# A windowed attention's probabilities turned by VectorE and bounced through DRAM, their low part taken by GpSimd, and weights loaded in pieces

## The reference

```
qkv = h @ w_qkv                      # h: gated x, 8 x 128 x 512
scores = einsum('bqhgd,bkhd->bhgqk', q, k) * 128**-0.5
bias = -slopes * sqrt(max(rel, 0)), -inf where rel < 0
attn = softmax(scores + bias)
out = einsum('bhgqk,bkhd->bqhgd', attn, v).reshape(8, 128, 4096)
x = x + out @ w_o
```

## Time and profile before

| | |
|---|---|
| device time, median of 3 runs | 2028.7 us (2025.08 to 2028.84) |
| device time of the profiled execution | 2021.16 us |
| its span | 2018.5 us |
| TensorE busy | 1966.2 us, 97% |
| VectorE, ScalarE, GpSimd busy | 76%, 65%, 47% |
| mean granted TensorE clock | 0.998 |

### The profile page before, as it was taken

One profiled execution on the slowest core, in us unless ns is written; L12 is line 12 of the kernel. 1 busy time (PEld: TensorE's weight loads), 2 busy tenths in 40 slices (PEclk: granted clock), 3 DMA queues, 4 the chain that ended last, 5 costly groups with the idle time before them and its releaser, 6 DMA issues.

```text
span 2018.5 us, 35965 instructions
## 1 busy us (share of the span) xinstructions
PE 1966.2 (97%) x12221; PEld 1669.4 (83%) x12221; DVE 1536.3 (76%) x3386; ACT 1317.0 (65%) x3796; POOL 940.4 (47%) x917
## 2 busy tenths in 40 slices
PE   7999999999999999999999999999999999999997
PEld 6777777888888888888888888888888888888774
DVE  6777765667666656688887887888878878888997
ACT  4676773545544545567777777777777777777785
POOL 3200014565665665644544544545445445454662
PEclk9999999999999999999999999999999999999999
DMA  7301102333433334412121121121211211212010
GB/s 263 100 28 48 54 1 82 118 100 95 140 96 97 123 102 77 129 42 82 32 64 53 33 84 32 32 84 32 64 53 33 84 32 32 84 33 84 29 31 37
DMA packets 91158, 142.21 MB, mean 70 GB/s; under 512 B 24914, under 2 KB 63058, under 8 KB 86498
## 3 DMA queue, kind: packets, MB, share of 16 engines
q1 hardware_dynamic: 69474, 89.55, 13.4%
q0 software_dynamic: 21504, 50.37, 8.7%
HBM read 119.93 MB, written 19.93 MB: 69 GB/s over the span
## 4 chain that ended last, share of the span: by engine, by line
PE 85%; DVE 7%; ACT 4%; DMA 2%; issue 2%; SPq 0%; POOL 0%; ACTq 0%; DVEq 0%
PE PS L1721 9%; PE PS L1733 9%; PE PS L1633 8%; PE PS L1499 8%; PE PS L1556 8%; PE PS L1706 6%; PE PS L1688 6%; PE PS L1647 4%; PE PS L1512 4%; PE PS L1691 3%; PE PS L345 3%; PE PS L1527 3%; PE PS L1542 2%; PE PS L501 1%; PE PS L1657 1%
## 5 line engine op out<-in xcount | busy, mean ns | idle before, releaser
L1304 POOL DMA_INDIRECT ffn_weights<-in_kcache,arena x256 | 259.8, 1015 | 78.0 <-issue 77.1
L2626 POOL DMA_INDIRECT vcache<-in_vcache,rows x256 | 249.9, 976 | 77.1 <-issue 55.6
L2475 ACT ACTIVATE pr<-pr,sm 128x640 f32<-128x640 f32 x256 | 209.4, 819 | 64.6 <-DVE sm L2085 64.4
L2101 DVE TENSOR_TENSOR prT_lo<-PS,prT_hi 128x512 fp32r<-128x512 f32 x320 | 208.8, 685 | 42.0 <-ACT prT_hi L2486 25.4
L2486 ACT ACTIVATE prT_hi<-PS 128x512 fp32r<-128x512 f32 x320 | 178.0, 597 | 67.9 <-PE PS L1706 67.8
L2085 DVE CUSTOM_DVE_ANT_0 pr<-PS,ffn_weights,sm 128x640 f32<-128x640 f32 x256 | 211.0, 878 | 0.5 <-PE PS L1691 0.5
L2632 POOL TENSOR_TENSOR vcached_lo<-vcache,vcached_hi 128x512 fp32r<-128x512 f32 x64 | 83.3, 1301 | 235.8 <-ACT vcached_hi L2457 235.8
L1706 PE MATMUL PS<-consts,pr 128*128 128x128 f32 x1280 | 172.1, 273 | 1.4 <-DVE prT_lo L2101 1.2
L1706 PEld LDWEIGHTS PS<-consts,pr 128*128 128x128 f32 x1280 | 149.6, 141 | 25.2 <-DVE prT_lo L2101 1.9
L1688 PE MATMUL PS<-kT_hi,qT_hi 128*128 128x320 f32 x512 | 155.2, 311 | 3.8 <-DVE sm L2085 2.4
L1688 PE MATMUL PS<-kT_lo,qT_hi 128*128 128x320 f32 x512 | 154.1, 309 | 0.0
(11 more groups left out here) (324 smaller groups left out, 6446.3 us busy)
## 6 DMA issues: line engine op xcount, KB each, us to landing
arena<-in_wqkv SPq DMA_DIRECT2D x16, 1536.0 KB
arena<-in_wo SPq DMA_DIRECT2D x16, 1024.0 KB
turned_keys<-ffn_weights POOLq DMA_DIRECT2D x64, 256.0 KB
kcache<-turned_keys SPq DMA_DIRECT2D x256, 64.0 KB
arena<-in_wcT SPq DMA_DIRECT2D x8, 1024.0 KB, 6.4
ffn_weights<-in_kcache,arena POOLq DMA_INDIRECT x256
vcache<-in_vcache,rows POOLq DMA_INDIRECT x256
arena<-in_xT SPq DMA_DIRECT2D x8, 256.0 KB, 7.8
```

Source lines behind the costliest of these rows:

```text
L1304: pool.indirect_dma_start(out=key_pages[:, n % 2, c, :], out_offset=None, in_=T["kcache"], in_offset=bass.IndirectOffsetOnAxis(ap=key_rows ...
L2101: dve.tensor_tensor(prT2[1][:, n % 3, :, :].rearrange("p h n -> p (h n)"), bank(4 + n % 2), prT2[0][:, n % 3, :, :].rearrange("p h n -> p ...
L2475: act.activation(pr2[:, h, :], pr2[:, h, :], ACT.Exp, bias=nm2[:, h:h + 1], scale=-1.0, accum_out=rs2[:, h:h + 1]).then_inc(a2_ex, 1)
L2626: pool.indirect_dma_start(out=vcache[:, c, :], out_offset=None, in_=T["vcache"], in_offset=bass.IndirectOffsetOnAxis(ap=rows[:, g, b, c:c ...
```

## The change

For items 8 to 54 (`TURNED`, 47 items) TensorE no longer turns the probabilities. VectorE transposes them in 32x32 blocks right after it has normalised them, SyncE stores the result to DRAM (256 KB, one transfer) and loads it back in four transfers of 64 KB so that the blocks land where a full transposition puts them; the queries then stand in the order (block, head, query), and `hi_of_o1` and `lo_of_o1` read them accordingly. ScalarE rounds the landed tile one step later than before, ahead of its copy of the turned key. The low part is taken by GpSimd instead of VectorE: in its list it stands behind the store of the step's last unit of keys and the first of the four gathers that follow it. `weigh1` of item i moves into TensorE's step i+1, between the second and the third quarter of the query head, and `project_out1` of item i into step i+2. The own values get a third buffer for that. The low parts of the output weights are taken in the second step of a group instead of the first. SyncE's list is written anew: the weights of a group come in pieces of 128 columns, spread over the steps behind each item's bounce. Items before 8 and behind 54 are handled as before, with one step of transition at item 55.

```diff
+        TURNED = range(B, ITEMS - B - 1)
+        probs_turned = fw[:, B * D + 4 * CACHED:B * D + 5 * CACHED].rearrange("p (c h n) -> p c h n", c=4, h=GH)
+        probs_landed = area(29696, GH * P)
+        probs_kept = nc.dram_tensor("turned_probs1", [len(TURNED), P, 4, P], F32).ap()
+        WC_USES = 32 * (B // 2)
+
+        def stored1(i):
+            return s_sc, 2 * B + 16 * (i - TURNED[0] + 1)
+
+        def landed1(i):
+            return s_wc[0], WC_USES + 16 * 4 * (i - TURNED[0] + 1)
+
+        def own_v1(part, n):
+            slot = (n - TURNED[0]) % 3 if TURNED[0] <= n <= TURNED[-1] + 2 else n % 2
+            return vo2[part][:, slot, :] if slot < 2 else prT2[0][:, 2, 2 + part, :]
+
+        def by_heads(ap, i):
+            return (ap.rearrange("p (a h n) -> p a h n", a=4, h=GH) if i in TURNED
+                    else ap.rearrange("p (h n) -> p h n", h=GH))
+
+        def o_parts(ap, i):
+            return ap.rearrange("p h (a n) -> p a h n", a=4) if i in TURNED else ap
+
+        def delayed_out1(i):
+            return (i - 1,) if i - 1 not in TURNED else (i - 2,) if i - 2 in TURNED else ()
...
-            def gather(n):
+            def gather(n, cs=range(CHUNKS)):
                 g, b = group_of(n)
                 wait(pool, s_kpt, n - 1)
-                for c in range(CHUNKS):
+                for c in cs:
...
+            def lo_of_probs1(i):
+                pool.wait_ge(a1_pTh, i + 1)
+                pool.tensor_tensor(prT2[1][:, i % 2, :, :].rearrange("p h n -> p (h n)"), probs_landed,
+                                   prT2[0][:, i % 2, :, :].rearrange("p h n -> p (h n)"),
+                                   ALU.subtract).then_inc(a1_pTl, 1)
...
-                    gather(n + 2)
+                    gather(n + 2, (0,))
+                for i in TURNED:
+                    if n == turns_in(i)[-1]:
+                        lo_of_probs1(i)
+                if n + 2 < ITEMS:
+                    gather(n + 2, (1, 2, 3))
...
+            def load_q_weights1(g, parts=range(GH)):
+                for r in parts:
+                    wait(sp, a1_wl, QPARTS * (g - 1) + r + 1)
+                    sp.dma_start(stage_qkv[:, :, r * P:(r + 1) * P],
+                                 T["wqkv1"][g, :, :, r * P:(r + 1) * P]).then_inc(a1_w, 16)
+
+            def load_kv_weights1(g):
+                wait(sp, a1_wl, QPARTS * g)
+                sp.dma_start(stage_qkv[:, :, GH * HD:QKV], T["wqkv1"][g, :, :, GH * HD:QKV]).then_inc(s_wc[1], 16)
+
+            def load_out_weights1(g, hs=range(GH)):
+                wait(sp, a1_wol, GH * g)
+                for h in hs:
+                    sp.dma_start(stage_out[:, h, :], T["wo1"][g, :, h, :]).then_inc(a1_wo, 16)
+
+            def bounce_probs1(i):
+                sp.wait_ge(a1_pT, i + 1)
+                kept = probs_kept[i - TURNED[0], :, :, :]
+                sp.dma_start(kept.rearrange("p c n -> p (c n)"),
+                             probs_turned.rearrange("p c h n -> p (c h n)")).then_inc(stored1(i)[0], 16)
+                sp.wait_ge(a1_pTl, i)
+                sp.wait_ge(*stored1(i))
+                for c in range(4):
+                    sp.dma_start(probs_landed[32 * c:32 * (c + 1), :].rearrange("p (a n) -> p a n", a=4),
+                                 kept[:, c, :].rearrange("(a j) n -> j a n", j=32)).then_inc(landed1(i)[0], 16)
+
             sp.wait_ge(s_ymm, B)
-            for g in range(G):
-                wait(sp, a1_wl, QPARTS * g)
-                sp.dma_start(stage_qkv.rearrange("p t n -> p (t n)"),
-                             T["wqkv1"][g, :, :, :].rearrange("p t n -> p (t n)")).then_inc(a1_w, 16)
-                wait(sp, a1_wol, GH * g)
-                sp.dma_start(stage_out.rearrange("p h n -> p (h n)"),
-                             T["wo1"][g, :, :, :].rearrange("p h n -> p (h n)")).then_inc(a1_wo, 16)
-                if g == 0:
-                    sp.wait_ge(s_x2, B)
-                    table(1)
-                if 3 <= g < 7:
-                    keep_units(2 * g - 6)
-                if 2 <= g < 6:
-                    load_units(2 * g - 4)
+            load_q_weights1(0)
+            load_kv_weights1(0)
+            load_out_weights1(0)
+            sp.wait_ge(s_x2, B)
+            table(1)
+            load_q_weights1(1)
+            load_kv_weights1(1)
+            load_out_weights1(1)
+            load_q_weights1(2)
+            load_kv_weights1(2)
+            for i in TURNED:
+                bounce_probs1(i)
+                g, b = group_of(i)
+                if b == 0 and 1 <= g < 5:
+                    load_units(2 * g - 2)
+                elif b == 1:
+                    if g + 2 < G:
+                        load_q_weights1(g + 2, (0,))
+                    if 2 <= g < 6:
+                        keep_units(2 * g - 4)
+                elif b in (2, 3, 4):
+                    load_out_weights1(g + 1, ((0,), (1,), (2, 3))[b - 2])
+                elif b in (5, 6) and g + 2 < G:
+                    load_q_weights1(g + 2, ((1, 2), (3,))[b - 5])
+                elif b == 7 and g + 2 < G:
+                    load_kv_weights1(g + 2)
...
-                project_out1(i - 1)
+                for n in delayed_out1(i):
+                    project_out1(n)
...
-                turn_probs1(i)
+                if i not in TURNED:
+                    if i - 1 in TURNED:
+                        weigh1(i - 1)
+                    turn_probs1(i)
                 if i + 1 in AHEAD:
                     scores1(i + 1)
                 elif i + 1 < ITEMS:
                     turn_k1(i + 1)
-                if n < ITEMS:
+                if i in TURNED:
+                    project_q_head(n, (1,))
+                    if i - 1 in TURNED:
+                        weigh1(i - 1)
+                    project_q_head(n, (2,))
...
-                weigh1(i)
+                if i not in TURNED:
+                    if i - 1 in TURNED:
+                        project_out1(i - 1)
+                    weigh1(i)
...
+            def turn_probs1(i):
+                dve.wait_ge(a1_n, i + 1)
+                if i - 1 in TURNED:
+                    dve.wait_ge(*stored1(i - 1))
+                dve.transpose(probs_turned.rearrange("p c h n -> p h c n"),
+                              pr1(i).rearrange("p (h c n) -> p h c n", h=GH, c=4)).then_inc(a1_pT, 1)
...
                 normalise1(i)
+                if i in TURNED:
+                    turn_probs1(i)
...
-                    add1(i - 1)
+                    for n in delayed_out1(i):
+                        add1(n)
                     lo_of_v1(i + 1)
-                    lo_of_probs1(i)
+                    if i not in TURNED:
+                        if i - 1 in TURNED:
+                            lo_of_o1(i - 1)
+                        lo_of_probs1(i)
...
-                act.wait_ge(a1_pT, i + 1)
-                act.activation(prT2[0][:, i % 2, :, :].rearrange("p h n -> p (h n)"), bank(4), ACT.Copy).then_inc(a1_pTh, 1)
+                if i in TURNED:
+                    act.wait_ge(*landed1(i))
+                    act.wait_ge(a1_pv, i - 1)
+                else:
+                    act.wait_ge(a1_pT, i + 1)
+                act.activation(prT2[0][:, i % 2, :, :].rearrange("p h n -> p (h n)"),
+                               probs_landed if i in TURNED else bank(4), ACT.Copy).then_inc(a1_pTh, 1)
...
+                if i - 1 in TURNED:
+                    hi_of_probs1(i - 1)
                 if i + 1 in AHEAD:
                     kT_copy1(i + 1)
-                hi_of_probs1(i)
+                if i not in TURNED:
+                    if i - 1 in TURNED:
+                        hi_of_o1(i - 1)
+                    hi_of_probs1(i)
```

More of the change, by code:

```diff
@@ L262, in build @@
         s_w0 = [sem(f"w{n}0_loaded") for n in ("q", "k", "v", "o_then_ffn_out")]
-        s_wc = [sem(f"adapter_loaded{i}") for i in range(2)]
+        s_wc = [sem(f"adapter_then_{what}_loaded{i}") for i, what in enumerate(("turned_probs1", "kv_weights1"))]
         s_wh0, s_wl0 = sem("weights0_hi"), sem("weights0_lo")
@@ L1586, in step1 @@
                     turn_k1(i + 1)
-                if n < ITEMS:
+                if i in TURNED:
[3 more added lines that the diff above has]
+                    project_q_head(n, (2,))
+                elif n < ITEMS:
                     project_q_head(n, (0, 1, 2) if i == 5 else (1, 2) if i > GH else (3,))
@@ L1900, in lo_of_o1 @@
                 dve.wait_ge(a1_oh, i + 1)
-                dve.tensor_tensor(o2[1][:].rearrange("p h n -> p (h n)"), bank(6),
-                                  o2[0][:].rearrange("p h n -> p (h n)"), ALU.subtract).then_inc(a1_ol, 1)
+                dve.tensor_tensor(o_parts(o2[1][:], i), by_heads(bank(6), i), o_parts(o2[0][:], i),
+                                  ALU.subtract).then_inc(a1_ol, 1)
             def step1(i):
@@ L1941, in step1 @@
                 else:
-                    add1(i - 1)
```

(35 more changed lines are left out.)

11 lines of the change are left out of this document (6 added, 5 removed).

## The result

The changed kernel takes 2036.01 us (median of 6 runs, 2032.55 to 2038.24), the kernel before, beside it, 2027.24 (6 runs): 1.0041 of the time before, 95% interval [1.0026, 1.0055], or 8.8 us more. Run twice more, it came to 1.0040 [1.0027, 1.0053] and 1.0060 [1.0046, 1.0075].

The account below looks back on a forecast made before the run. The prediction took TensorE, busy 97% of the span, to bound the kernel. Its terms, -21.9 + 24.6 + 7 + 1.4 = +11 us on the median 2028.7, gave 2040 us, with an 8-in-10 range of 2008 to 2058.

Parts of the forecast that it names:

- TensorE is the bound, and the transpositions are gained in full: Items 8 to 55: removing TensorE's transpositions (20.7 us) and 1.2 us of idle time gains 21.9 us; step 8.66 us.
- The six holes: Steps behind items 13, 21, 29, 37, 45, 53: TensorE waits 4.1 us each for GpSimd's low part, 24.6 us in all.
- The clock: Behind each of six TensorE waits, half clock costs 1.2 us, 7 us in all; bounds 0 and 1.7 each.
- The bounce: Store to DRAM and loads back, each turned item: 6.1 us, hidden in about one step of 8.6 us.
- The other bound, 4.3 us: Transfer time in traffic, read as a wait behind the last gather; it would make store and loads 10.7 us, 2.1 too many.
- Start: Step 9 has no output projection, so the first store and load have less cover: between 0 and 2.8 us, taken as 1.4.
- pieces: SyncE's 16 and 16 large weight transfers become pieces, asked for at least three steps before use: counted as nothing.
- VectorE and ScalarE at nothing: Stage of items 8 to 55: VectorE swaps a 692 ns subtraction for a 699 ns transposition, ScalarE still copies one tile: no cost.
- The sum: Whole kernel: -21.9 + 24.6 + 7 + 1.4 = +11 us on the median 2028.7, giving 2040 us.
- All hidden: Rival: the low part of items 13, 21, ... is ready when TensorE asks; 2008 us, chance 0.17.
- GpSimd the bound: Rival: GpSimd's gathers run at 1.27 us instead of 1.02, 22 us on top; 2062 us, chance 0.08.
- Late bounce: Rival: store and loads need over 8.6 us in every step, which becomes as long; about 2072 us at 9.5, chance 0.13.

Follow-up runs that it names:

- planned list: The changed kernel with GpSimd's low parts placed by a build-time plan where they are ready, between two gathers of a unit if need be: 2014.62 us, ratio 0.9938.
- the first experiment: The changed kernel with GpSimd's low part behind the store and first gather of the step's first unit of keys, also in double steps: 2046.49 us, ratio 1.0117.
- timed pair: The changed kernel with 15 unused products ahead of the weighing in six double steps, 2027.53 us, against the changed kernel on the same chip, 2034.78 us.
- the longer bounce: The kernel with the low part on VectorE, plus one or two unread 256 KB stores ahead of each bounce: 2059.78 us (1.0158) and 2130.55 us (1.0521).

## Why the prediction was right, point by point

**TensorE is the bound, and the transpositions are gained in full.** Right in kind, a little too large. The step is 8.66 us as worked out. With the holes out of the way the stretch from item 8 to attention 2 went from 518.6 to 500.9 us, -17.7, where the terms -21.9 and +1.4 give -20.5. Most of the 2.8 us between is idle time that was counted as gone: the stretch had 2.2 us of it before and has 3.6 now.

**The six holes.** Predicted 6 x 4.1 = 24.6 us, at the weighing behind items 13, 21, ..., 53; measured 22.7 (21.7 and 23.2 in the repeats), 3.6 to 4.3 each, at just these places. The arithmetic of the stores and gathers held: S+0.9 to S+10.7 is 9.8 us, measured 9.5.

**Why they are there.** Here a sentence of the prediction was wrong: that GpSimd "has no earlier moment for it". The planned list found one between the second and the third gather of the first unit. Also, the place in the list is only half of it. A unit takes GpSimd 667.32 - 661.18 = 6.14 us, a low part with its gap 1.44. In a double step and the next that is 3 x 6.14 + 2 x 1.44 = 21.3 us of work in 2 x 8.66 = 17.3 us. GpSimd is 4.0 us late by then, wherever the low part stands, and in each later step it wins back 8.66 - 7.58 = 1.1 us, so it is level after four more. I had summed its work over eight steps (68.0 of 69.3 us), and called the store behind the hole late "by about a microsecond"; I did not sum it over two. What a list can choose is who is late: behind the second unit the low part of the double step is, behind the first unit the next low part (the first experiment), and in the planned list the stores of keys, for which nobody waits in five of the six places.

**The clock.** Predicted 1.2 us a hole, 7 in all, between bounds of 0 and 1.7. The timed pair shows 1.2 (7.25), the chain behind the first hole 1.8, the profiles with filled and open holes 1.7 (10.2 in all) and about 1.25 (7.5). Single holes lost 1.4 to 3.1 us behind them, so the upper bound was too low for one hole, though not for their mean in the timed pair. The reason given, that part of the half-rate stretch lies in the hole itself, is borne out in four of the six and not in the first two.

**The bounce.** Predicted 6.1 us, measured 0.03 + 2.08 + 1.74 and 2.2 for the landing of the loads (the last from the longer bounce) = 6.1, and hidden. That is a fast one; the store alone took 2.6 us in the mean. Its room was overstated: ScalarE reaches the tile 654.04 - 646.54 = 7.5 us behind the transposition, not 8.6. The prediction has two times for that moment, S+3.7 in the part on the bounce and, with ScalarE's part ready at S+3.1, about S+2.5 in the part on GpSimd; the second was right. The margin is about 1.4 us, and one bounce of the changed kernel did come 1.1 us late, by a store of over 4 us. So that the bounce stayed hidden was a closer thing than the prediction's reckoning, with 2.5 us to spare, says. The other bound, 4.3 us, was misread: 666.91 in the earlier trace rows is no gather but GpSimd's own 256 KB store of keys, which is as near in size as the row that was taken.

**Start, pieces, other engines.** Predicted 1.4 us at the start; the waits list has one of 1.0 there. The pieces, counted at nothing, are worth 2.6 us on the kernel before. Only 8 and 8 of the large transfers became pieces, not 16 and 16: the others belong to attention 2. VectorE and ScalarE at nothing: right, beyond the 1.0 us at the start and the one late bounce no wait of TensorE stands for them.

**The sum.** +11 us predicted, on 2028.7; +8.8 measured, on 2027.24. By the stage marks: -17.7 + 22.7 + 10.2 = +15.2, against 16.3 seen in the profiles. With the clock's price of the timed pair it is -17.7 + 22.7 + 7.25 = +12.3. The timed differences were 8.8 in the first pair, 7.9 and 13.2 in the repeats, so from one group to the next the difference of two medians strays by 5 us, and the sum lies inside. That 2036 came out so near to 2040 is in part luck: the gain was put 2.8 us too high and the holes 1.9 too high, which nearly cancel. The range given for the forecast itself doesn't add up at its upper end either: holes of 4.8 us at the full clock price make 2047 to 2049, not 2052.

**The rivals.** All hidden: not in this kernel, but its argument, that GpSimd has enough free time in the stage, was sound, and the planned list gave 2014.62 us. GpSimd the bound: no, its gathers took 0.99 us in the mean (1.02 before) and its subtraction 1.29 (1.30 before). The rule of shared interfaces for which the prediction cites the Trainium skill (GPSIMD Engine Reference, "1. Specifications") cost nothing that can be seen in these means. Single instructions agree with it: with the low part behind the first unit, and in the planned list, five and six of the 47 subtractions took 2.05 us or more, all of them beside VectorE's low part of 128x1024 weights. Late bounce: not so, but its price was worked out wrongly; when the bounce did grow by one store, of 3.7 us in the mean, the steps grew by 1.0 to 1.2, not by the whole excess over the room.

**A version that beats both.** The bounce with the low part on VectorE: 0.9903 and 0.9928 of the time before. The planned list, with GpSimd keeping the work, comes to 0.9938.

## What to carry to other kernels

Sum the work of an in-order engine over the densest two steps, not only over the whole period: the predicted 98% over eight steps hid 123% over two. When such an engine is late for a while, decide which of its jobs is late: put work that the bound engine waits for in front, even into the middle of a unit, and let stores slip that nobody reads soon; then look at the waits again, since the planned list still had one of 5.1 us. And give a new wait on the critical path to the engine with room in every step (here VectorE at 78%), not to the one whose mean share is lowest.

## What the runs showed of the hardware

A hole of 3.6 to 4.3 us in TensorE's work at the full clock cost between a third and a half as much again (1.2 to 1.7 us on 3.8, in the mean of six): the granted clock was 0.62 in the 4 us behind the start of the first weighing after one, and the chain lost 1.8 us there. The Trainium skill (TensorE: Matmul & The Clock Gate, "Why this matters for your kernels") advises against idle gaps between bursts, and these holes agree with it; the remaining waits of 1 us in the same stage, and those of 0.9 to 2.7 us in the kernel with six low parts on VectorE, left the clock at 1.00. Products that nobody reads, put in place of the holes, made the kernel 7.25 us faster.

A 256 KB store from SBUF to DRAM that SyncE issued within 1 us behind its weight pieces landed after 3.4 to 5.4 us, one issued 2.5 us or more behind them after 2.2 to 2.8 (26 and 11 of the 47 first stores of the longer bounce). That isn't all that delays one: in the changed kernel a store issued 3.9 us behind the last piece took over 4 us. GpSimd's subtraction of a 128x512 tile takes 1.29 us, and took 2.06 beside VectorE's subtraction of 128x1024 with both operands in SBUF.
